# Key norms turned back into a PSUM bank, rounded from there by ScalarE and split by VectorE in one pass

## The reference

```python
def l2norm(t):
    return t / jnp.maximum(jnp.linalg.norm(t, axis=-1, keepdims=True), 1e-12)
def attn_layer(x, Wqkv, qs, ksc, Wo):
    ...
    q = l2norm(q) * qs
    k = l2norm(k) * ksc
    ...            # rotary tables on q and k
    out = local_attention(q, k, v)
    return out.transpose(0, 2, 1, 3).reshape(b, n, INNER) @ Wo
for i in range(DEPTH):
    x = attn_layer(shift_tokens(x), ...) + x
    x = ffn_layer(shift_tokens(x), ...) + x
```

## Time and profile before

| | |
|---|---|
| median of 3 runs | 3347.05 us (3346.89 to 3353.05) |
| the profiled execution, its own time | 3375.36 us |
| its span | 3373.6 us |
| busy share of the span | PE 86%, PEld 55%, DVE 88%, ACT 61%, POOL 72% |
| instructions | PE 57914, DVE 4200, ACT 3820, POOL 1679 |
| mean granted TensorE clock | 0.938 |

### The profile page before, as it was taken

One profiled execution on the slowest core, in us unless ns is written; L12 is line 12 of the kernel. 1 busy time (PEld: TensorE's weight loads), 2 busy tenths in 40 slices (PEclk: granted clock), 3 DMA queues, 4 the chain that ended last, 5 costly groups with the idle time before them and its releaser, 6 DMA issues. The chain is left out here.

```text
span 3373.6 us, 132100 instructions
## 1 busy us (share of the span) xinstructions
PE 2905.4 (86%) x57914; PEld 1846.3 (55%) x57914; DVE 2981.4 (88%) x4200; ACT 2061.4 (61%) x3820; POOL 2425.2 (72%) x1679
## 2 busy tenths in 40 slices
PE   5788889989989899987767788998999988999987
PEld 3455555655655555653323455565566655565653
DVE  6789899999999899896898878989999989899994
ACT  3466566666666665664764456666666666566663
POOL 3678777787787687774454667778788787787773
PEclk8899999999999999998887889999999999999998
DMA  5233332333333333320001333333343333333330
GB/s 140 65 83 73 82 91 68 89 90 72 86 92 71 84 85 71 83 72 28 7 7 44 80 72 79 75 87 86 75 97 76 90 84 72 81 94 71 86 76 14
DMA packets 114726, 250.85 MB, mean 74 GB/s; under 512 B 27244, under 2 KB 60648, under 8 KB 114152
## 3 DMA queue, kind: packets, MB, share of 16 engines
q1 hardware_dynamic: 114152, 242.40, 30.3%
HBM read 37.82 MB, written 3.15 MB: 12 GB/s over the span
## 5 line engine op out<-in xcount | busy, mean ns | idle before, releaser
L1085 ACT ACTIVATE squares<-general 128x512 f32<-128x512 f32 x768 | 453.9, 597 | 720.8 <-PE general L658 712.2
L1279 POOL TENSOR_TENSOR probs<-probs,row_sum 128x1024 f32<-128x1024 f32 x192 | 365.3, 1903 | 426.3 <-DVE row_sum L957 425.5
L1259 POOL TENSOR_TENSOR q_ring<-q_ring,partner 128x512 f32<-128x512 f32 x384 | 491.1, 1279 | 216.6 <-DMA partner<-sines 216.3
L868 DVE SCALAR_TENSOR_TENSOR sines<-general,vec,consts 128x512 f32<-128x512 f32 x768 | 560.7, 730 | 68.4 <-ACT squares L1085 65.5
L1259 POOL TENSOR_TENSOR k_ring<-k_ring,partner 128x512 f32<-128x512 f32 x384 | 490.8, 1278 | 0.0
L692 PE MATMUL general<-probs_t,v_buf 32*64 32x64 f32 x24576 | 339.4, 236 | 158.3 <-issue 87.0
L656 PE MATMUL general<-xs_hi,wqkv_lo 128*128 128x512 f32 x768 | 457.3, 595 | 15.8 <-DVE xs_lo L897 7.6
L692 PEld LDWEIGHTS general<-probs_t,v_buf 32*64 32x64 f32 x24576 | 305.6, 135 | 248.8 <-issue 241.7
L1273 POOL TENSOR_TENSOR probs<-probs,q_scale 128x1024 f32<-128x1024 f32 x192 | 365.3, 1903 | 15.1
L668 PE MATMUL general<-att,wo 128*128 128x512 f32 x768 | 370.4, 627 | 6.5 <-ACT att L1155 5.2
L719 PE MATMUL general<-k_ring,q_ring 64*32 64x64 f32 (+1 forms) x24576 | 294.2, 224 | 88.4 <-issue 53.5
(11 more groups left out here) (232 smaller groups left out, 6348.2 us busy)
## 6 DMA issues: line engine op xcount, KB each, us to landing
partner<-sines SPq DMA_DIRECT2D x1536, 128.0 KB, 2.3
wqkv_raw<-in_wqkv SPq DMA_DIRECT2D x80, 208.0 KB, 2.7
wo<-in_wo SPq DMA_DIRECT2D x12, 512.0 KB, 5.1
w<-in_w SPq DMA_DIRECT2D x12, 341.0 KB, 3.2
base_dram<-x SPq DMA_DIRECT2D x8, 256.0 KB, 2.4
att<-in_wqkv SPq DMA_DIRECT2D x2, 1024.0 KB, 6.1
sines<-base_dram SPq DMA_DIRECT2D x8, 256.0 KB, 4.0
w<-in_w SPq DMA_DIRECT2D x12, 128.0 KB
```

What stands on the lines that cost most here:

```text
L868: e.scalar_tensor_tensor(out=by_seq(sines[:, i % 2, which, :]), in0=g, scalar=scale, in1=both(tables[:, 2 * which + 1, :]), op0=ALU.mult, ...
L1085: e.activation(squares[:, (2 * p + which) % 4, :], general_of(("proj", k, n, p, which))[:, :], ACT.Square).then_inc(S[f"squared_{side}"], 1)
L1259: e.tensor_tensor(y, y, partner[:, i % 2, which, :], ALU.add).then_inc(S[f"rotated_{side}"], 1)
L1279: e.tensor_tensor(y, y, spread_keys(row_sum[:, i % 2, :]), ALU.mult).then_inc(S["probs_done"], 1)
```

## The change

- `norm_t` gets its second copy of the root from ScalarE: one more square root of 128 by 128 into the second quarter of the tile, ahead of the one in place. The `q_scaled` semaphore counts nine per item.
- VectorE no longer rounds and subtracts. It transposes the tile straight into a bank of the ring, key `("back", k, n)`, which is taken at the start of step p = 1, ahead of the q projection's.
- ScalarE copies that bank, rounded to float32r, into `inv_hi` (the place of its call is the one that the old copy had).
- VectorE then writes `inv_parts` in one scalar_tensor_tensor: `inv_hi` times a column of constants (-1 in the rows of the low half, 0 elsewhere) plus the bank. The call stands right behind `dve_norms_back`.
- The selection matrix takes its rows from the first two quarters instead of the second and third.

```diff
+            if st.norms_back is not None:
+                self.use(("back", k, st.norms_back), "inv_parts", k * ITEMS + st.norms_back + 1)
...
         def dve_norms_back(e, w, k, n):
-
             m = k * ITEMS + n
             w.wait_ge(S["k_root"], m + 1)
-            root, low, high = (norm_t[:, :, i * NORM_ROWS:(i + 1) * NORM_ROWS] for i in range(3))
-            e.tensor_copy(high.bitcast(F32R), root).then_inc(S["norms_high"], 1)
-            w.wait_ge(S["norms_high"], m + 1)
-            e.tensor_tensor(low, root, high, ALU.subtract).then_inc(S["norms_low"], 1)
-            w.wait_ge(S["norms_low"], m + 1)
-            w.wait_ge(S["inv_parts"], m)
-            e.transpose(inv_norm[:, :], norm_t.rearrange("p w h -> p (w h)")).then_inc(S["k_norms_turned"], 1)
+            w.wait_ge(S[BANKS.free(("back", k, n))[0]], BANKS.free(("back", k, n))[1])
+            e.transpose(general_of(("back", k, n))[:, :], norm_t.rearrange("p w h -> p (w h)")).then_inc(S["k_norms_turned"], 1)
             turned["norms"] = m + 1
+
+        def dve_norms_low(e, w, k, n):
+            m = k * ITEMS + n
+            w.wait_ge(S["inv_hi"], m + 1)
+            w.wait_ge(S["norm_spread"], m * GROUPS)
+
+            e.scalar_tensor_tensor(out=inv_parts[:, :], in0=inv_hi[:, :].bitcast(F32), scalar=low_rows, in1=general_of(("back", k, n))[:, :],
+                                   op0=ALU.mult, op1=ALU.add).then_inc(S["inv_parts"], 1)
...
                 if st.norms_back is not None:
                     dve_norms_back(e, w, k, st.norms_back)
+                if st.norms_back is not None:
+                    dve_norms_low(e, w, k, st.norms_back)
...
-            w.wait_ge(S["q_scaled"], (m + 1) * 8)
+            e.activation(norm_t[:, :, NORM_ROWS:2 * NORM_ROWS], norm_t[:, :, 0:NORM_ROWS], ACT.Sqrt).then_inc(S["q_scaled"], 1)
+            w.wait_ge(S["q_scaled"], (m + 1) * 9)
             e.activation(norm_t[:, :, 0:NORM_ROWS], norm_t[:, :, 0:NORM_ROWS], ACT.Sqrt).then_inc(S["k_root"], 1)
 
         def act_norms_high(e, w, k, n):
             m = k * ITEMS + n
             w.wait_ge(S["k_norms_turned"], m + 1)
-            w.wait_ge(S["norm_spread"], m * GROUPS)
-            e.activation(inv_parts[:, :], inv_norm[:, :], ACT.Copy).then_inc(S["inv_parts"], 1)
+            w.wait_ge(S["inv_parts"], m)
+            e.activation(inv_hi[:, :], general_of(("back", k, n))[:, :], ACT.Copy).then_inc(S["inv_hi"], 1)
```

More of the change, by code:

```diff
@@ L57 @@
 C_IDENT, C_CENTER, C_MEAN, C_SUMSEL = 0, P, 2 * P, 2 * P + 1
-C_TABLES = C_SUMSEL + 64
+C_LOW = C_SUMSEL + 64
+C_TABLES = C_LOW + 1
 C_STAY = C_TABLES + 4 * SEQ
@@ L251, in use @@
         self.last[at] = (sem, value)
-        self.written[at] = key[0] in ("proj", "v", "spread", "scores", "project", "ffn_out", "center", "var")\
+        self.written[at] = key[0] == "back" and self.filled[key] or key[0] in ("proj", "v", "spread", "scores", "project", "ffn_out", "center", "var")\
             or key[0] in ("gate", "value") and HIDDEN_CUTS[key[3]][1] == P
@@ L365 @@
 xs_hi xs_lo proj_q proj_k squared_q squared_k cos_q cos_k sin_q sin_k moved0 moved1 rotated_q rotated_k
-squares_summed sums_kept sums_turned sums_inverted q_scaled k_root norms_high norms_low k_norms_turned inv_parts
+squares_summed sums_kept sums_turned sums_inverted q_scaled k_root k_norms_turned inv_hi inv_parts
 v_projected v_kept norm_spread k_inv_kept mask_set scored k_norms_off row_max max_off q_norms_off exponent row_sum row_inv
@@ L394, in macaron_kernel @@
         mean = consts[:, C_MEAN:C_MEAN + 1].broadcast_to([P, P])
+        low_rows = consts[:, C_LOW:C_LOW + 1]
         tables = consts[:, C_TABLES:C_TABLES + 4 * SEQ].rearrange("p (i t) -> p i t", i=4)
@@ L414, in macaron_kernel @@
         partner = sb("partner", [P, 2, 2, COLS])
-        inv_norm = sb("inv_norm", [P, COLS])
+        inv_hi = sb("inv_hi", [P, COLS], F32R)
         norm_t = sb("norm_t", [P, ITEM_WINS, WIN])
@@ L1664, in constants @@
     c[np.arange(P), C_SUMSEL + 30 + np.arange(P) // DH] = 1
+    c[np.arange(P) % WIN // NORM_ROWS == 1, C_LOW] = -1
     half = np.arange(0, DH, 2, dtype=f)
@@ L1689, in constants @@
             row = norm_row(head // 2, 1) + head % 2
-            c[row + NORM_ROWS, at:at + WIN] = c[row + 2 * NORM_ROWS, at:at + WIN] = 1
+            c[row, at:at + WIN] = c[row + NORM_ROWS, at:at + WIN] = 1
     return c
```

## The result

| | before | changed |
|---|---|---|
| median of runs | 3350.05 us (4 runs) | 3466.89 us (3463.48 to 3477.51, 4 runs) |
| ratio, 95% interval | | 1.0328 [1.0287, 1.0369] |
| span of the profiled execution | 3373.6 us | 3475.7 us |
| DVE busy | 2981.4 us | 2892.0 us |
| mean granted clock | 0.938 | 0.927 |

What follows compares the result with a forecast made beforehand. Three nearly full engines (DVE, PE, POOL) handing work to each other were taken to bound each item. Gap 100 us plus clock 42, less 20 for slack, gave 122 on 3347: median 3469 us, range 3395 to 3515.

Steps and rivals of the forecast that it cites:

- The new wait: PE at step p = 1: v waits for `inv_parts` and starts 2.8 to 3.0 us late in nearly every item.
- the q projection's new wait: PE at p = 1: q projection waits for the k rotation of p = 0; at most 7 us, taken as 0.
- classes: 42 items grouped by PE's idle time until p = 2 ends: 2.8, 2.6, 2.2 or 0.5 us stay, 100 us in all.
- slack that could not be placed: Later steps of an item where PE and DVE both wait for an undelayed chain: 20 us taken off.
- The clock: PE behind the gap ahead of v: two in three of 37 gaps bring a clock fall costing 1.7 us, 42 us.
- DVE's work: DVE per item: cast and subtraction go, one 0.75 us pass comes; -2.0 us per item, -97 us in all.
- The one that ended on the other side, faster: DVE's lost work counts if the pass ends before PE reaches v: 3250 or 3287 us; chance 0.05.
- The first rival: Gap ahead of v partly absorbed, clock stays up behind most gaps: 50 to 85 us more, 3415 us; chance 0.27.
- The fourth, no change: V's delay lies beside a wait of DVE's in all classes, so the time stays the same; chance 0.03.
- Every gap brings a fall and nothing is absorbed: All gaps ahead of v count in full, each with a clock fall: 100 + 63 = 163 us, 3510 us; chance 0.15.

Runs made afterwards that it cites:

- E1: Changed kernel with only back's bank taken later, just behind the output projection, so that the spread and not v inherits the wait: 3383.52 us, ratio 1.0037.
- E4: Changed kernel with eight matmuls, result thrown away, between the k projection and v of step 1 to keep PE busy: 3437.38 us, ratio 1.0199.
- e2: Changed kernel with back's bank taken behind the output projection and DVE's pass moved behind the k rotation: 3350.97 us, ratio 0.9949.
- e6: Kernel before without DVE's subtraction of 1862 ns per item, so only the rounded key norms are used: 3332.95 us, ratio 0.9918.
- e5: Bank behind the output projection, pass behind the k rotation, and DVE's transpose of the probabilities ahead of that rotation in step 1: 3353.38 us, ratio 0.9988.
- e9: Changed kernel with bank behind the output projection, ACT's copy ahead of the square of k, DVE's pass between addition to x and k rotation: 3353.02 us, ratio 0.9935.

## Why the prediction was right

**The new wait.** The prediction's step was that v gets the bank of `back` and so waits for `inv_parts`, 2.8 to 3.0 us, nearly the same in every item. Measured 2.8 us in the mean of 42 items and 2.66 in the item worked out, with the releaser named. E1 moves only the bank, and 2.9 of 3.3% go. One small term was taken as nothing: PE comes to the k projection 0.17 us later in its item than before, 7 us in all, which is the most that the prediction had allowed for the q projection's new wait.

**What stays of it.** By classes 100 us were to stay without the clock, less 20 for slack that could not be placed: 80. E4 puts this part at 67 us. The classes themselves were too large. They took as slack only the idle time of PE, up to the values of step 2, and left 100 / 42 = 2.4 us per item; in e4, with the clock up, the values come 1.3 us late and the row sum 1.5 us, 63 us over 42 items. So the slack of which 20 us were taken off lies within step 2, ahead of the row sum, and not at later steps as the prediction supposed: behind the row sum e4 loses nothing that can be told from its 67 us. PE's idle time did not show all of it. In the 20 items that have less than 0.1 us of it, the stretch from v to the values takes mostly 6.8 us before; in nearly all items of e4, with the same instructions at full clock, it takes 6.2 to 6.3 us. So about half a microsecond of waiting seems to be counted as busy there. With the falls in it, the row sum slips by 3.0 us per item, 126 us over 42, of which 102 us arrive at the end of the profiled execution; where the rest is taken back was not tried. Outside the falls near v the items have 36 falls instead of 42, which may be a part of it.

**The clock.** Two in three of 37 gaps were to bring a fall of 1.7 us, 42 us. There were falls behind 34 of 42 gaps, a third more than forecast, and by e4 the 41 falls that the filling removed cost 43 us together, a little over 1 us each, well below 1.7. The errors in number and price went in opposite directions, and the measured 43 is uncertain by 18: that the two products agree to 1 us is luck. That gaps of this kind cost clock, and roughly how much, is shown. The rule of the Trainium skill, "TensorE: Matmul & The Clock Gate", section "HAM oscillation — how this bites in real kernels", is borne out in the main: 34 of the 42 gaps brought a fall, though not each of them, and filling the idle time of PE, with matmuls whose result nobody reads, made the kernel faster by 1.3%.

**The number.** Forecast were 122 us more, 80 and 42; the ratio makes it 110, 67 and 43. That the medians 3469 and 3466.89 lie 2 us apart is closer than the working deserves.

**DVE's work.** -97 us of busy time were forecast, -89.4 measured on the page; added up instruction by instruction, with overlaps counted twice, it is -96.0. The pass was to take 0.75 us and was never stretched: 746 to 750 ns in all 48. The transpose into PSUM took 723 ns, 0.71 had been taken. The port rule of "SBUF — State Buffer" (the Trainium skill), "SBUF: two separate sides", agrees: the pass, with one input in PSUM, ran beside an operation of POOL's in 45 of 48 cases without being held, while the old subtraction ended 0.15 us behind the POOL operation under way in all 48.

**The rivals.** The one that ended on the other side, faster, named as its condition that v's bank be another one. E1 is that case with nothing else changed, and is 12 us slower; with the pass moved too, e2, it is 17 us faster. Neither gives the 60 to 97 us that were priced. The price let DVE's busy time count nearly in full, where e6 shows that a third comes through. The first rival, a partly absorbed gap without falls at 50 to 85 us, had the absorption right (67 us) and the falls wrong (34 instead of few). The fourth, no change, asked that v's delay lie beside a wait of DVE's; the row sum is 1.5 us late even with the clock up. "Every gap brings a fall and nothing is absorbed" (3510) fell by the absorption and by the price of a fall rather than by their number.

## What to carry to other kernels

In a ring of buffers a new user does not only need a buffer: the one who comes a full ring later inherits its release. Count forward from the new place to see who that is, and choose the place so that the heir is somebody who needs the same result anyway (here the spread instead of v): the same computation went from 3.3% slower to 0.5% faster by that and one moved call. Price a wait on TensorE twice, once for the gap and once for the clock behind it; and do not price work taken from the fullest engine by its busy time while three engines stand above 90% within an item. Nor is an engine without idle time in the trace without slack: here half of a delay of 2.9 us was taken back within one step, where PE's idle time had shown 0.8 us in the mean.

## What the runs showed of the hardware

A DVE subtraction of 128 by 128 elements from two SBUF operands took 1.86 us on the mean and in all 48 cases ended 0.15 us after the POOL operation that was under way; the new pass from SBUF and PSUM, over four times as many elements, was never stretched (748 ns). That the stall counts as busy time is worth knowing: e6 removed this instruction, 89 us of busy time, and gained 27 us.

With PE kept busy in the gap, the items had 29 falls of the clock in all, fewer than the 42 of before: falls later in the item went away too, which had not been expected. E1, e2, e5, e6 and e9, which leave PE's instructions alone, also have 31 to 35. Why the later ones thin out was not tried.
